# Second attention layer: rounding of the feed-forward weights and the ends of the norms move from VectorE to GpSimd

## The reference, cut to what matters

```python
x = layernorm(x + mamba(x))                       # its norm is done inside the stage below
x = layernorm(x + attention(x, ctx, mask))        # 16 heads, 361 keys
x = layernorm(x + ffn(x))

def _weight_fake_quant(w):                        # w_gate, w_up: 704 x 256; w_down: 256 x 704
    scale = jnp.max(jnp.abs(w), axis=1, keepdims=True) / QMAX
    return jnp.clip(_ste_round(w / scale), -QMAX - 1.0, QMAX) * scale

def _layernorm(x, axis=-1, eps=1e-05):
    m = jnp.mean(x, axis=axis, keepdims=True)
    v = jnp.var(x, axis=axis, keepdims=True)
    return (x - m) / jnp.sqrt(v + eps)
```

## Time and profile before

| What | us |
|---|---|
| Median of 3 runs | 1338.29 (1337.8 to 1340.01) |
| Span of the profiled execution, first to last instruction | 1336.9 |
| What lies between that span and the median | 1.4 |
| VectorE busy, of the span | 1095.1 (82%) |
| GpSimd busy, of the span | 821.0 (61%) |
| TensorE busy, of the span | 1155.3 (86%) |
| ScalarE busy, of the span | 828.6 (62%) |

### The profile page before, as it was taken

The page is one execution under the profiler, slowest core; times in us unless marked ns, Lnnn a source line. Parts: engine busy times, 40 slices in busy tenths (PEclk is TensorE's granted clock), DMA queues, the critical chain, the costliest instruction groups (busy, mean ns, idle before and its releaser), DMA issues.

```text
span 1336.9 us, 17670 instructions
## 1 busy us (share of the span) xinstructions
PE 1155.3 (86%) x6026; PEld 672.1 (50%) x6026; DVE 1095.1 (82%) x1618; ACT 828.6 (62%) x1827; POOL 821.0 (61%) x743
## 2 busy tenths in 40 slices
PE   7798888878588999989989899899987888888874
PEld 4555555544244544545545455455454555555544
DVE  3577777575889999999999999999999768776556
ACT  2555555565477677866777668776754365566564
POOL 6001111100698998988989989899899344455405
PEclk9899999988889999999999989999897999999975
DMA  6000002000602305015041060230500300100000
GB/s 203 13 12 13 12 12 71 1 1 5 226 8 94 147 1 198 17 48 193 1 169 45 1 241 1 94 120 1 198 31 0 80 17 17 32 17 2 1 1 25
DMA packets 22142, 79.15 MB, mean 59 GB/s; under 512 B 4935, under 2 KB 8847, under 8 KB 21138
## 3 DMA queue, kind: packets, MB, share of 16 engines
q1 hardware_dynamic: 22054, 78.02, 16.8%
HBM read 76.77 MB, written 1.24 MB: 58 GB/s over the span
## 4 chain that ended last, share of the span: by engine, by line
PE 38%; DVE 33%; POOL 10%; ACT 10%; issue 7%; DMA 0%; SPq 0%; ACTq 0%; DVEq 0%; POOLq 0%
PE ps L637 36%; DVE ps L1954 10%; POOL arena L1868 6%; DVE arena L1959 4%; DVE arena L1957 4%; DVE hstat L1097 4%; ACT arena L872 3%; POOL arena L1880 2%; ACT ps L1751 2%; PE ps L708 2%; DVE arena L1917 2%; ACT L632 1%; ACT arena L882 1%; DVE arena L1085 1%; DVE arena L1063 1%
## 5 line engine op out<-in xcount | busy, mean ns | idle before, releaser
L637 PE MATMUL ps<-arena 128*32 128x100 f32 (+8 forms) x3300 | 521.0, 383 | 81.7 <-ACT arena L872 26.1
L1868 POOL TENSOR_TENSOR arena<-arena 128x1600 f32<-128x1600 f32 x128 | 456.4, 3580 | 35.4 <-DVE ps L1954 27.2
L637 PEld LDWEIGHTS ps<-arena 128*32 128x32 f32 (+6 forms) x3300 | 262.3, 146 | 298.2 <-issue 109.2
L637 PE MATMUL ps<-arena,ident 128*128 128x400 f32 x1024 | 386.2, 528 | 29.3 <-POOL arena L1880 19.6
L1751 ACT ACTIVATE ps<-arena 128x400 f32<-128x400 f32 x512 | 282.9, 590 | 184.5 <-DVE arena L1957 151.3
L1954 DVE TENSOR_TENSOR_SCAN ps<-ps,arena 128x800 f32<-128x800 f32 x176 | 320.6, 1822 | 22.7 <-ACT ps L1751 17.0
L637 PEld LDWEIGHTS ps<-arena,ident 128*128 128x128 f32 x1024 | 201.9, 200 | 197.6 <-issue 29.2
L872 ACT ACTIVATE arena<-ps,hstat 100x361 f32<-100x361 f32 x256 | 143.6, 563 | 107.1 <-DVE hstat L1097 107.0
L610 POOL TENSOR_SCALAR stat<-stat 100x1 f32<-100x1 f32 (+1 forms) x44 | 8.6, 196 | 289.8 <-DVE stat L591 288.6
L1957 DVE TENSOR_TENSOR arena<-ps,arena 128x800 f32<-128x800 f32 x176 | 174.4, 991 | 6.0
L1097 DVE TENSOR_REDUCE hstat<-ps 100x2 f32<-100x722 f32 x128 | 115.7, 905 | 68.7 <-PE ps L637 68.2
(11 more groups left out here) (191 smaller groups left out, 1000.9 us busy)
## 6 DMA issues: line engine op xcount, KB each, us to landing
arena<-bc_scratch SPq DMA_DIRECT2D x64, 800.0 KB, 6.7
arena<-in_ctxT SPq DMA_DIRECT2D x16, 361.0 KB, 4.1
arena<-in_w_in SPq DMA_DIRECT2D x4, 1024.0 KB, 4.9
arena<-in_expT SPq DMA_DIRECT2D x1, 2048.0 KB, 12.6
arena<-in_w_out SPq DMA_DIRECT2D x4, 512.0 KB, 3.2
arena<-in_mask SPq DMA_DIRECT2D x8, 141.0 KB
arena<-in_xT SPq DMA_DIRECT2D x2, 400.0 KB, 3.9
x_tok<-in_x_tok SPq DMA_DIRECT2D x1, 800.0 KB
```

Of the source, the lines that this page charges most:

```text
L637: return nc.tensor.matmul(outp, lhsT, rhs, start=first, stop=last)
L1868: nc.gpsimd.tensor_tensor(bx[:, unit % BX].rearrange("p (j t) -> p j t", j=SEGMENT), bbc[:, nq].rearrange("p (j t) -> p j t", j=SEGMENT), ...
```

## The change: what it does

Four things change, all in the second attention.

1. The six parts of `quantise_weight` that round, clamp and cast leave VectorE. GpSimd does them as `quantise_piece` in 18 pieces, one at the last step of each of 18 quads in a row (steps 23, 27, ... 91). Piece 0 of three rounds half a matrix, piece 1 clamps it, piece 2 casts it to bf16. The three parts with the scales stay on VectorE at their steps 19, 43 and 67 (`weight_scale`).
2. The second half of both norms, (z - mean) x root, goes from VectorE to GpSimd (`norm_end_pool`), directly behind the root.
3. The attention's norm is written to `x_tok` directly, which saves the copy L1243. TensorE and the maximum L1241 read it there.
4. VectorE gets waits ahead of its statistics, because GpSimd still reads the slots of the norm two before.

```diff
+        PEAKS_AT = (H + 3, 2 * H + 11, 4 * H + 3)
+        PIECES_AT = range(H + 7, H + 7 + 18 * QUAD, QUAD)
...
+        def norm_end_pool(pool, par, z, dst, done):
+
+            pool.wait_ge(n_root, norms.rooted)
+            st = stat[0:S, par]
+            nc.gpsimd.tensor_scalar(dst, z, st[:, 6:7], st[:, 9:10], ALU.subtract, ALU.mult).then_inc(done, 1)
...
-                        pe_turn(pe, a, b, "FT", a.x2[0:S, b % 2])
+                        pe_turn(pe, a, b, "FT", x_tok[:, b, :])
...
                     for b in pre(g, AT["1x"]):
                         norm_root(pool, b % 2)
+                        norm_end_pool(pool, b % 2, a.x1[0:S, b % 2], a.x1[0:S, b % 2], a.in_ready)
                     for b in pre(g, AT["1xe"]):
                         gp_residual(pool, a, b)
                     for b in fin(g, AT["1N"]):
                         norm_root(pool, b % 2)
+                        norm_end_pool(pool, b % 2, a.zt[0:S, b % 2], x_tok[:, b, :], a.x_ready)
+                    if g in PIECES_AT:
+                        quantise_piece(pool, PIECES_AT.index(g))
...
             a.wait_read(dve, b, "O")
+            if a.layer == 1:
+                dve.wait_ge(a.in_ready, min(b + 3, B))
+                wait(dve, a.x_ready, b - 1)
             norm_start(b % 2, z)
...
             step(nc.vector.tensor_tensor(t, x_tok[:, b, :], xm[:, b, :], ALU.add))
+            wait(dve, a.in_ready, b - 1)
+            wait(dve, a.x_ready, b - 3)
             norm_start(b % 2, t)
...
-                    for b in pre(g, AT["1xe"]):
-                        norm_end(dve, b % 2, a.x1[0:S, b % 2], a.x1[0:S, b % 2], a.in_ready)
+                        norms.ended += 1
...
-                    for b in fin(g, AT["1Ne"]):
-                        norm_end(dve, b % 2, a.zt[0:S, b % 2], a.x2[0:S, b % 2], a.x_ready)
+                        norms.ended += 1
...
-                    if g >= H + 3 and (g - H - 3) % 8 == 0 and (g - H - 3) // 8 < 9:
-                        quantise_weight(dve, (g - H - 3) // 8)
+                    for w in range(3):
+                        if g == PEAKS_AT[w]:
+                            weight_scale(dve, w)
...
-                        vstep.mark(V.tensor_reduce(axm[0:S, b:b + 1], a.x2[0:S, b % 2], AX.X, ALU.max,
-                                                   apply_absolute_value=True))
-                        V.tensor_copy(x_tok[:, b, :], a.x2[0:S, b % 2]).then_inc(a.out_ready, 1)
+                        V.tensor_reduce(axm[0:S, b:b + 1], x_tok[:, b, :], AX.X, ALU.max,
+                                        apply_absolute_value=True).then_inc(a.out_ready, 1)
...
+        def quantise_piece(pool, k):
+
+            G_ = nc.gpsimd
+            w, k = divmod(k, 6)
+            half, pass_ = divmod(k, 3)
+            f, q, _, inv, n = weights[w]
+            h = slice(half * n // 2, (half + 1) * n // 2)
+            if pass_ == 0:
+                pool.wait_ge(f_scaled, w + 1)
+                for c in range(half * n // 2, (half + 1) * n // 2):
+                    last = G_.tensor_scalar(f[:, c], f[:, c], inv[:, c:c + 1], ROUND, ALU.mult, ALU.add)
+                last.then_inc(f_round, 1)
+            elif pass_ == 1:
+                pool.wait_ge(f_round, 2 * w + half + 1)
+                G_.tensor_scalar(f[:, h], f[:, h], ROUND + QMAX, ROUND - QMAX - 1, ALU.min, ALU.max).then_inc(f_clamp, 1)
+            else:
+                pool.wait_ge(f_clamp, 2 * w + half + 1)
+                G_.tensor_scalar(q[:, h], f[:, h], -ROUND, 1.0, ALU.add, ALU.mult).then_inc(f_wq, 1)
```

More of the change, by code:

```diff
@@ L2059, in decoder @@
         f_mean, f_shift = sem("f_mean"), sem("f_shift")
+        f_scaled, f_round, f_clamp = sem("f_scaled"), sem("f_round"), sem("f_clamp")
         f_stored = [sem(f"f_stored{k}") for k in range(4)]
@@ L2185, in ffn_pool @@
                                         ALU.add).then_inc(f_shift, 1)
-        def quantise_weight(dve, part):
-            V = nc.vector
-            w, part = divmod(part, 3)
-            f, q, scale, inv, n = ((wg_f[0:IP], wg_q[0:IP], sg, rg, IC), (wu_f[0:IP], wu_q[0:IP], su, ru, IC),
-                                   (wd_f, wd_q, sd, rd, KD))[w]
-            if part == 0:
-                if w == 0:
-                    dve.wait_ge(ld_ffn, 16 * 4)
-                step(V.tensor_reduce(scale, f, AX.X, ALU.max, apply_absolute_value=True))
-                step(V.tensor_scalar(scale, scale, 1.0 / QMAX, None, ALU.mult))
-                step(V.reciprocal(inv, scale))
-                return
-            for c in range((part - 1) * n // 2, part * n // 2):
-                vstep.mark(V.tensor_scalar(f[:, c], f[:, c], inv[:, c:c + 1], ROUND, ALU.mult, ALU.add))
-            h = slice((part - 1) * n // 2, part * n // 2)
-            vstep.settle()
-            step(V.tensor_scalar(f[:, h], f[:, h], ROUND + QMAX, ROUND - QMAX - 1, ALU.min, ALU.max))
-            V.tensor_scalar(q[:, h], f[:, h], -ROUND, None, ALU.add).then_inc(f_wq, 1)
+        weights = ((wg_f[0:IP], wg_q[0:IP], sg, rg, IC), (wu_f[0:IP], wu_q[0:IP], su, ru, IC),
+                   (wd_f, wd_q, sd, rd, KD))
@@ new lines, in weight_scale @@
+        def weight_scale(dve, w):
+            f, _, scale, inv, _ = weights[w]
+            if w == 0:
+                dve.wait_ge(ld_ffn, 16 * 4)
+            step(nc.vector.tensor_reduce(scale, f, AX.X, ALU.max, apply_absolute_value=True))
+            step(nc.vector.tensor_scalar(scale, scale, 1.0 / QMAX, None, ALU.mult))
+            nc.vector.reciprocal(inv, scale).then_inc(f_scaled, 1)
+        def quantise_piece(pool, k):
[15 more added lines that the diff above has]
+                G_.tensor_scalar(q[:, h], f[:, h], -ROUND, 1.0, ALU.add, ALU.mult).then_inc(f_wq, 1)
```

## The result

The median is 1345.89 us (1333.53 to 1349.68, 20 runs), and of the kernel before, measured beside it, 1338.34 us (1331.46 to 1345.96, 20 runs). The ratio is 1.0044, 95% interval 1.0026 to 1.0063: slower by 0.4%, or by 3.5 to 8.4 us. The medians are 7.55 us apart, where 8.5 was predicted; single executions of one kernel lie up to 16 us apart. The profiled execution has a span of 1343.1 us, 6.2 more than before.

A forecast was written before the change was run, and what follows sets the result against it. GpSimd's order in A and B quads was to set the pace, with VectorE's rounding on the chain before. Forecast 1338.29 + 13.8 added on GpSimd - 5.3 removed from VectorE = 1346.8 us; range 1336 to 1358, its own 1341 to 1353.

The forecast's parts named there:

- the search's 1.03: Quads 10 to 11: lateness from one scale search that stays on VectorE, 7.25 against 6.22 us without it.
- the 0.72: Quads 17, 18: lateness of the other scale search on VectorE, already paid before the change, 0.72 us.
- What the change takes away, 5.3: Quads 5 to 21: rounding leaves VectorE, removing 2.37 + 1.19 + 1.19 + 0.56 = 5.3 us of lateness.
- The three prices: On GpSimd: norm end 1.23 us (1.35 with semaphore), rounding 1.83, clamping 1.05 and casting 1.1.
- norm end is cheap: Rival: GpSimd's norm end takes 0.46 us instead of 1.23, added sum 6.0, time 1339.0 us; chance 0.16.
- rounding and casting dear: Rival: both cost 4.05 ns an element on GpSimd, 20.8 us more, time 1367.6 us; chance 0.09.
- Idle time covers it: Rival: GpSimd's room in A and B quads holds norm end and piece, nothing added, time 1333.0 us; chance 0.12.
- the cover: Quad 26: how late GpSimd's first scaled head may be before TensorE's transposes wait for it, 0.86 us.
- The walk: Quads 25, 26: GpSimd's instructions summed without a gap from root to scaling, 1.61 + p + q later.
- p and q: Times of the pieces GpSimd runs ahead of the scaling, p in the A quad, q in the B quad.
- its 0.75: Each full A and B pair: lateness left after the cover, before pieces are added, 0.75 us.
- the blocking: Quads 25, 26: GpSimd's norm end holds VectorE's L1091 and second maximum through the shared port; 0.9 taken instead of 0.75.

The follow-up runs named there:

- e7: Kernel after, with transposes of two tiles repeated 3 to 12 times in A and B quads to fill TensorE's waits; stage 166.18 us, whole time 1344.35 us.
- e2: e1 with the norm ends back on VectorE, without the new waits ahead of the statistics; median 1329.7 us against 1340.14 before, ratio 0.9923.
- e1: Kernel after with all 18 pieces moved ahead of C and D quads only; stage 155.51 us, median 1333.36 us against 1340.14 before, ratio 0.9955.
- e6: Kernel after with GpSimd's norm end multiplying by the root and 1.0, mean not subtracted; stage 160.43 us, whole time 1341.91 us.
- e9: e3 with two tiles' transposes repeated 3 to 6 times in A quads, 3 in B quads; stage 159.27 us, whole time 1330.62 us.
- e10: e2 with the repeated transposes of e9, as a control; stage 157.20 us, median 1333.35 us against 1339.76 before, ratio 0.9954.
- e3: Kernel after with the norm ends back on VectorE, pieces on GpSimd where the change put them; stage 161.71 us, whole time 1339.67 us.
- e4: Kernel after with the rounding back on VectorE, norm ends on GpSimd; stage 165.79 us, whole time 1340.47 us.
- e8: e4 with two tiles' transposes repeated 4 to 8 times in A quads, 3 to 4 in B quads; stage 162.70 us, whole time 1345.17 us.

## Why the prediction was right

**The result** came within a microsecond (7.55 against 8.5), and that closeness is luck: the interval reaches from 3.5 to 8.4 us. The mechanism was right. GpSimd's order of work set the pace of the A and B quads, as predicted. The pairs of quads show how far the terms hold. The table has the lateness over the clean 12.08, in us. In quads 9 and 10 the search's 1.03 is taken off. In 17 and 18 the 0.63 is counted in by which quad 16, with its search, was longer than 7.40; the 0.72 for it is taken off the sum:

| Quads | predicted | after | e7, clock kept from quad 9 on |
|---|---|---|---|
| 5, 6 | 1.8 | 1.4 | 1.4 |
| 9, 10 | 3.6 | 3.5 | 3.3 |
| 13, 14 | 2.9 | 2.6 | 2.6 |
| 17, 18 (search included) | 2.8 | 2.3 | 2.2 |
| 21, 22 | 2.5 | 3.1 | 2.2 |
| 25, 26 | 0.9 | 0.3 | 0.4 |
| Sum less the search of 0.72 | 13.8 | 12.6 | 11.4 |

**What the change takes away, 5.3.** It came off. Quads 8 and 12 fell from 8.59 to 7.40, quad 20 from 7.71 to 7.40, and C quads took 5.75 to 5.81 (5.79 to 5.81 before). In the B quads it is hidden behind the norm ends; e2, without them, has 6.23 in quads 6, 14 and 18, where the kernel before had 7.41, 7.41 and 6.47. Only the searches still hold a quad (quad 16 took 8.03). Taking the norm end off VectorE was put at nothing. In e1 it gave a little: quads 5, 6 and 17, 18 took 11.80 and 11.83, up to 0.3 less than clean.

**The three prices.** Right within 0.1 us each. Taking the price from the one instruction of the same form, and not from its nearest kin, was the choice that decided: e6 shows that with the other one the stage would have taken 160.43, as before, which is the rival "norm end is cheap" (it said 7.8 less, the stage showed 6.9). That rival, and "rounding and casting dear", are refuted by the groups of the profile.

**Idle time covers it.** Refuted for A and B quads, by the pairs of the table and by waits for the scaling of 15.2 us instead of 10.3, and true for C and D quads, by e1. GpSimd's idle time in an A quad plus the cover is 1.4 us. Norm ends alone fit it (e1 has them there, and its pairs are at most 0.4 us over the clean 12.08, the search apart); pieces alone nearly do; both do not. With the repeats in both, pieces in A and B quads cost 2.1 us when the norm ends are on VectorE (e9 159.27, e10 157.20). When the norm ends are on GpSimd they cost about 9.0 (e7 166.18, less e1's 155.51 and 1.7 for the repeats).

**The walk.** It was right to let it run without a gap. The pair without pieces, 25 and 26, shows what was mis-sized: 0.9 was predicted, and 0.34 us measured, at full clock. GpSimd there, in the kernel after:

```profile
1236.19 0.19 POOL L618 TENSOR_TENSOR stat<-stat 100x1 f32<-100x1 f32 x1
...
1237.70 1.11 POOL L985 TENSOR_SCALAR arena<-arena,hstat 100x361 f32<-100x361 f32 x2
1238.78 0.72 POOL L990 TENSOR_TENSOR x_tok<-arena,bob 100x256 f32<-100x256 f32 x1
1239.49 1.10 POOL L985 TENSOR_SCALAR arena<-arena,hstat 100x361 f32<-100x361 f32 x2
1240.68 0.19 POOL L612 TENSOR_SCALAR stat<-stat 100x1 f32<-100x1 f32 x1
...
1242.43 0.19 POOL L618 TENSOR_TENSOR stat<-stat 100x1 f32<-100x1 f32 x1
1242.74 1.22 POOL L631 TENSOR_SCALAR x_tok<-arena,stat 100x256 f32<-100x256 f32 x1
1243.94 2.35 POOL L985 TENSOR_SCALAR arena<-arena,hstat 100x361 f32<-100x361 f32 x4
```

From the root's end at 1236.38 to the end of the first head at 1244.51 it took 8.13 us. The prediction's sum for this is 1237.03 - 1228.47 = 8.56 (p and q at zero). So the walk was 0.43 too long, a little in almost every term: the second scaling 1.24 against 1.10 (its own row had 1.11), the bias 0.80 against 0.71, the first scaling 0.04, the two norm ends 0.06 together, and 0.10 for the start of two pieces that are not there. With 0.43 less, its 0.75 becomes 0.32, which is what the pair lost. So the cover of 0.86 was right. The same 0.75 stands in the pairs from 9 to 22, which came out 0.3 to 0.6 lower than predicted with the clock kept.

The other 0.15 in this pair was the blocking, "a 1.23 us norm end can hold L1091 and the second maximum in the same way" (VectorE's L1103 is the L1091 of before). In quads 25 and 26 no norm end held either. VectorE and GpSimd in quad 21:

```profile
1208.05 1.23 POOL L631 TENSOR_SCALAR arena<-arena,stat 100x256 f32<-100x256 f32 x1
1208.12 0.23 DVE L1103 TENSOR_SCALAR hstat<-hstat,anyv 100x2 f32<-100x2 f32 x1
...
1208.25 0.90 DVE L1109 TENSOR_REDUCE hstat<-ps 100x2 f32<-100x722 f32 x1
...
1209.27 0.85 POOL L2225 TENSOR_SCALAR arena<-arena 128x704 f32<-128x704 f32 x1
...
1209.48 0.67 DVE L1103 TENSOR_SCALAR hstat<-hstat,anyv 100x2 f32<-100x2 f32 x1
```

and in quad 14:

```profile
1160.06 1.22 POOL L631 TENSOR_SCALAR x_tok<-arena,stat 100x256 f32<-100x256 f32 x1
```

```profile
1160.84 0.47 DVE L1103 TENSOR_SCALAR hstat<-hstat,anyv 100x2 f32<-100x2 f32 x1
```

In quad 21 L1103 starts 0.07 us behind the norm end, takes its usual 0.23 us, and the maximum its 0.90. Under the rounding piece L1103 takes 0.67 and ends when that does. In quad 14 L1103 starts 0.78 us into the norm end, takes 0.47 and ends when that does. In quad 17 it starts 0.67 us into the norm end and takes 0.23. So a norm end can hold L1103, but not at every moment, and it cost at most 0.24 us at a time in the kernel after. The maximum was never held. The Trainium skill (SBUF — State Buffer, section "Who interferes with whom") says that whoever issues first keeps the shared pair for the whole instruction, and that a tensor_reduce never contends. The rows agree on the maximum, on the rounding and on quad 14; in quad 21 a norm end in flight left L1103 alone, which does not follow from it, and here the measurement decides.

**What was not in it: the clock.** In the kernel after it costs between 1.2 us of the stage (e7) and an estimated 2.9, of one execution each. It is smaller there than in e3 and e4, and 1.0 us of it lies in quads 21 and 22. The predicted sum was 1.2 above the measured one with the clock's cost inside, and 2.4 above e7's. So the agreement is partly two errors that offset each other: the walk's small terms and the blocking were priced too dear, and the clock was missing. Both are small beside the walk's 11.4, which is e7's sum and holds what the repeats themselves cost. The prediction named the price of the pieces, then the cover, as what would break its sum most; both held. That the clock's share is smaller in the kernel after than in e4, which does less on GpSimd, is shown by the distances of 11.3 to 12.6 us above: GpSimd's longer row hides the slow scores.

## What to carry to other kernels

Idle time of an engine is not one pool. It is a slot ahead of each thing that is waited for, and two additions that each fit can together miss it. Place the addition behind the last instruction that another engine waits for: the same 18 pieces lost 7 us at even distances and gained 5 at chosen ones. (Those 7 and 5 us are of the stage in one execution each; the medians of e1 and the kernel after lie 6.8 below and 7.55 above the kernel before.) And price an instruction by a row with the same operations, even if there is only one in the trace.

## What the runs showed of the hardware that was not expected

- **A wait of TensorE can cost twice.** Behind 2.25 us of idle time in quad 9 it ran at 0.50 of full speed for the 2.84 us of the scores and the mask, and on into quad 10. In quad 21 it stood 1.27 us, and the scores behind it took 1.54 us as well. The three quads 28 to 30 took 17.15 us at full clock and 20.98 at 0.76. Writing tiles again in the wait shortened e4's stage by 3.1 us and e3's by 2.4, though e8 then lost 2.6 us behind the stage. e2 had a wait of 0.76 to 0.78 us at the same place in quads 9, 17 and 21, and only quad 17 had a lowered clock, so a single wait does not tell it. The Trainium skill (TensorE: Matmul & The Clock Gate, Part 1) says that the clock has two values only and goes by how busy TensorE was recently, and that frequent short idle times can make it swing. The rows at 0.50 and 1.00 agree, and so do e8 and e9.
- **On GpSimd the pair of operations sets the price.** 100x256 with subtract and multiply takes 1.22 us, with multiply and multiply 0.48 (one scalar per row) or 0.55 (two). Multiply-add, min-max and add-multiply took 0.48 us for 88x256, 1.04 for 88x1024 and 1.04 with the cast to bf16. Multiply-min is dear as well, with 0.44 us for 128x64. The Trainium skill's rough line-rate for one-input work (GPSIMD Engine Reference, "Engine selection") fits the cheap forms roughly (VectorE clamped 88x1024 in 0.70 us, GpSimd in 1.04) and fails for the dear ones.
- **The dear form held VectorE's two-element instruction in part only**: not when that started 0.07 or 0.67 us into it (0.23 us, quads 21 and 17), but at 0.78 us (0.47, quad 14). The rounding form of 0.85 us, and before the change L982 of 0.72 us, held it until they were done.
